# Gated mixing moved into the gather loop of a graph attention, on one core of a Trainium2 chip

## The chip, the cores and the metric

The kernel runs on one core of one Trainium2 chip. The core has five engines with queues of their own: TensorE (PE: matmuls; PEld is its weight load), VectorE (DVE), ScalarE (ACT), GpSimd (POOL) and SyncE (SP, which here only issues DMAs and passes signals). They meet at semaphores. The metric is the device time of one execution in microseconds; less is better.

## What is computed

Two layers over a graph of 6250 nodes and 206250 edges (sorted by destination), each: a graph operator plus a mixing operator, added to x, then a mixture of experts. The change is about the first layer's first half:

```
xn = layernorm(x)
x  = x + gnn(xn, edges) + mix(xn)

gnn:  h = xn @ W                       (8 heads of 32)
      e = leaky_relu(a1[src] + a2[dst])
      alpha = softmax of e over the edges of one destination
      out[dst] = sum over edges of h[src] * alpha   (+ bias)

mix:  context = softmax(K, over nodes)^T V          (one 32x32 block a head)
      out  = Q context
      gate = sigmoid(gelu(layernorm(xn) @ Wg1 + bg1) @ Wg2 + bg2)
      result = (out * gate) @ Wproj + bproj
```

Both are to within float32 accuracy; nothing of this differs between the two kernels.

## The kernel before

**Stages.** The program is a row of blocks, each ended by a barrier of all engines. `opening` reads x, writes the rows h (`h_dram`) and the turned, normalised x (`xt_dram`), and folds Q and the context into one matrix `wqc`. `mix_out` does the gated mixing alone. `attend` is the attention. Then come the experts, the relation rows, the relations' gather (`relations`, which like `attend` uses `report_groups` and `gather_groups`) and the last experts.

**`mix_out`** goes over the 49 blocks of 128 nodes in quads (four blocks, 512 columns), 13 of them. PE computes the hidden gate (`psG`), x times `wqc` (`psQ`) and the gate (`psV`); ACT does Gelu and Tanh; DVE multiplies (line 810); PE projects per block (line 753); DVE adds x and the bias (line 793) and SP stores to `x_dram`. x was read into `k.xb` by `opening`; POOL adds the biases to it and, once a block is done, sets its part of `k.xb` to zero (line 709, 49 memsets), because `attend` sums into `k.xb`.

**`attend`** first makes tables on DVE in a block of its own (lines 978 to 988), then the row of numbers `psN` on PE in another (`numbers`), and then runs the loop. Edges come in 202 groups of 1024 (8 tiles of 128). POOL gathers the rows h[src] of a group by 8 indirect DMAs (line 868) into a ring of 7 groups. A *step* handles a pair of a group and a block of destinations: 250 steps, T = 202 + 49 - 1. Four steps make a *turn* (U = 4).

In step t the engines work for several steps at once. DVE: waits `turned` (of PE's transposes); small operations on the maxima (1131 to 1164), ending in the exponents' arguments `arg`; with them `fade` (line 1108), which scales a block's sums by the correction of step t-1; then `hot` (1168, which destination each edge has, for step t+3), `scan` (1172), `add_up` (1113, adds the sums of step t-1 from `psS`), the edge types' part of the messages (1178), and the messages (1182). ACT: Exp of `arg` into the bank `psW` (1009), stages the next gathered rows (1015), and makes `hot_t` in two passes (1021, 1023). PE: first half of the sums of step t (1042), `spread_nodes` (915), the logits `psL` (1063, waits DVE's `shifts`), the maxima `psX` (1071, waits DVE's `marked`), two transposes (1076, 1080, which signal `turned`), and the second half of the sums.

**Written out or in a loop.** Each engine runs turns 1 to 61 as a hardware loop, `Fori(1, z.T // U)`. Steps -5 to 3 ahead of it and the last two steps, 248 and 249, are written out. In the loop, PE and DVE read the numbers of groups and blocks into registers once a turn (`Ahead`). Written-out steps read them with `one_of` wherever they are used. On PE that is inside the loop over j:

```
for j in range(G):
    pe.matmul(psL_v[:, j, :, :], hot_t[...],
              split[:, ds(block_no(2) * LW, LW)], ...)
```

so `block_no(2)` is read 8 times. `v.drain()` holds DVE's next instruction until all before it are done.

Of the kernel before, what the change touches and what calls it, by code (L numbers as in the profile page):

```python
# [5 lines left out]
P = 128  # L6
# [73 lines left out]
class Sizes:  # L80
# [4 lines left out]
    def __init__(self, n, e):  # L85
# [11 lines left out]
        self.NCH = -(-(self.T + 3 * U) // P)  # L97
        self.COLS = self.NGT * G
# [56 lines left out]
def opening(nc, z, S, k, mean, rstd, rstd2, ratio, wqc):  # L155
# [10 lines left out]
    with ExitStack() as c:  # L166
# [21 lines left out]
        blocks = sb("blocks", [P, nch * P], I32)  # L188
# [33 lines left out]
        with nc.Block() as block:  # L222
            @block.sync
            def _(sp):
# [11 lines left out]
                sp.dma_start(k.src_at[:], S["src"]).then_inc(of_late, 16)  # L236
# [7 lines left out]
                for b in range(NB):  # L244
# [10 lines left out]
                    if b == tables_at + 4:  # L255
                        sp.wait_ge(tab2, 16 * 2 * nch)
                        lines = k.table_dram.rearrange("q n o -> q (n o)")
                        sp.dma_start(k.last_pair[:], lines[0:1, :]).then_inc(tab3, 16)
                        sp.dma_start(k.pair_block[:], lines[1:2, :]).then_inc(tab3, 16)
                        sp.dma_start(blocks[:], lines[1, :].partition_broadcast(P)).then_inc(tab3, 16)  # L260
# [15 lines left out]
            def _(p):  # L276
# [12 lines left out]
                p.iota(k.pair_group[:], [[1, nch * P]], base=0, channel_multiplier=0)  # L289
# [300 lines left out]
        with nc.Block() as block:  # L590
            @block.vector
# [41 lines left out]
def mix_out(nc, z, k, S, wqc, ratio):  # L633

    NB = z.NB
    GH = S["L0_mix_Wg1"].shape[1]
    quads = [(lo, min(lo + 4, NB)) for lo in range(0, NB, 4)]
    NQ = len(quads)  # L640
    with ExitStack() as c:
        sem = c.enter_context(semaphores(nc, "mo_"))
        sb = lambda n, s, d=F32: c.enter_context(nc.sbuf_tensor("mo_" + n, s, d))
        xt = sb("xt", [P, NB, C])
        g1 = sb("g1", [P, KC, GH])
        g1s = sb("g1s", [P, KC, GH])
        g2 = sb("g2", [GH, C])
        wp = sb("wp", [P, KC, C])
        cols = sb("cols", [P, 3, KC])
        half = sb("half", [P, KC])  # L650
        bg1 = sb("bg1", [GH, 1])
        bg = sb("bg", [GH, 1])
        bias = sb("bias", [P, 2, C])
        hid = sb("hid", [GH, 2, 4 * P])
        gate = sb("gate", [P, KC, 4 * P])
        prod = sb("prod", [P, 2, KC, 4 * P])
        new = sb("new", [P, 4, C])
        psG = c.enter_context(nc.psum_tensor("mo_psG", [GH, 2, 512], F32))
        psQ = c.enter_context(nc.psum_tensor("mo_psQ", [P, KC, 512], F32))
# [2126 lines left out]
```

## Time and profile before

| what | us |
|---|---|
| median of 3 runs | 6431.17 (6430.95 to 6431.87) |
| the profiled execution, its own time | 6432.53 |
| its span in the profile | 6430.7 |
| granted TensorE clock, mean | 0.885 |
| opening | 0 to 249 |
| mixing alone (`mix_out`) | 249 to 409 |
| `attend`, tables and row of numbers | 410 to 419 |
| `attend`, first gather to last sum | 419.8 to 2509.0 |
| experts of the first layer | 2510 to 3070 |
| relation rows | 3070 to 3912 |
| relations and what is behind | 3912 to 6431 |

The stages' ends were read off the timeline of instructions; the profiled execution took 1.8 us more than its span, which lie around it. In the attention (420 to 2510) the engines' busy times are PE 1596.5, DVE 1823.0, ACT 697.3 and POOL 1532.4 us. A busy time there says little by itself: POOL is never idle for long, though it counts as busy 73% only, since 0.30 us stand between two of its gathers.

### The profile page before, as it was taken

Reading aid. Unit: us, or ns where it says so; the run is one execution under the profiler, and the core shown is the slowest. Engines: PE = TensorE matmul, PEld = TensorE weight load, DVE = VectorE, ACT = ScalarE, POOL = GpSimd, SP = SyncE. Lnnn points to the kernel's source line nnn. Section 1 sums busy time; section 2 is a strip of 40 time slices with the busy share of each in tenths; the row PEclk is TensorE's granted clock in tenths of the full one; section 3 lists DMA queues with packets and bytes.
Section 4 is the critical chain, followed back from the end, with each engine's and each line's share of the span. In section 5 each row is a group of like instructions: output and inputs, shape, how many; then the busy total and the mean of one; then the engine's idle time right before and its main releaser. Section 6 shows DMA issues by size and latency. Waiting matters only on the chain. (4 is left out here: it accounts for less than half of the span.)

```text
span 6430.7 us, 105194 instructions
## 1 busy us (share of the span) xinstructions
PE 4977.0 (77%) x26438; PEld 3591.3 (56%) x26691; DVE 4128.9 (64%) x9565; ACT 1548.3 (24%) x3076; POOL 3649.1 (57%) x3844
## 2 busy tenths in 40 slices
PE   5867777777777776799799997777777777766694
PEld 4535555555555555798544444655555555555583
DVE  5438999998989898435650003877777777666444
ACT  1213333333333333454433331000000000000341
POOL 3447777777777773603200004777777777776524
PEclk8978999989888887799999998888888888888597
DMA  4424444444444443423344443333333333333345
GB/s 144 125 72 109 113 113 113 113 113 113 113 113 113 113 112 117 143 77 103 106 149 169 174 171 126 109 109 109 109 109 109 109 109 109 106 105 96 131 147 151
DMA packets 367220, 762.40 MB, mean 119 GB/s; under 512 B 92003, under 2 KB 232321, under 8 KB 354241
## 3 DMA queue, kind: packets, MB, share of 16 engines
q0 software_dynamic: 175104, 491.59, 27.1%
q1 hardware_dynamic: 184912, 262.86, 12.1%
q10 hardware_dynamic: 7056, 6.43, 0.3%
q8 instruction: 39, 0.64, 0.0%
q14 instruction: 109, 0.89, 0.0%
HBM read 562.75 MB, written 199.66 MB: 119 GB/s over the span
## 5 line engine op out<-in xcount | busy, mean ns | idle before, releaser
L868 POOL DMA_INDIRECT rg_ring<-y_dram,src_at x1612 | 1528.3, 948 | 1265.2 <-POOLq L906 774.3
L868 POOL DMA_INDIRECT ga_ring<-h_dram,src_at x1612 | 1532.6, 951 | 507.9 <-issue 460.8
L1716 PE MATMUL rg_psS<-rg_ring,rg_hot_w 128*128 x4000 | 1148.1, 451 | 397.7 <-SPq L844 304.2
L1716 PEld LDWEIGHTS rg_psS<-rg_ring,rg_hot_w 128*128 128x128 f32 x4000 | 902.0, 230 | 640.2 <-issue 478.1
L1042 PE MATMUL ga_psS<-ga_msg,ga_hot 128*128 128x280 f32 x4000 | 1194.1, 455 | 46.1 <-DVE ga_msg L1182 38.1
L1042 PEld LDWEIGHTS ga_psS<-ga_msg,ga_hot 128*128 128x128 f32 x4000 | 850.0, 221 | 313.9 <-DVE ga_msg L1182 88.6
L1833 DVE TENSOR_SCALAR rg_hot_t<-rg_psB,pair_node,place 128x1024 bf16<-128x1024 f32 x253 | 338.4, 1338 | 586.0 <-PE rg_psB L915 586.0
L1521 PE MATMUL rr_psY<-rr_wr,rr_xt 128*128 128x512 f32 x1568 | 675.1, 593 | 4.6 <-DMA rr_xt<-x_dram 4.6
L1182 DVE SCALAR_TENSOR_TENSOR ga_msg<-ga_psW,ga_ring 128x2112 f32<-128x2112 f32 x251 | 587.3, 2340 | 0.0
L1521 PEld LDWEIGHTS rr_psY<-rr_wr,rr_xt 128*128 128x128 f32 x1568 | 298.4, 190 | 379.0 <-issue 373.9
L2261 PE MATMUL f_psH<-f_xt,f_now 128*128 128x128 f32 x2688 | 351.3, 281 | 48.9 <-DVE f_now L2554 37.9
L1800 DVE TENSOR_TENSOR rg_picked<-rg_psL,rg_rel 128x384 f32<-128x384 f32 x251 | 138.9, 553 | 359.5 <-PE rg_psL L1723 333.9
L2261 PEld LDWEIGHTS f_psH<-f_xt,f_now 128*128 128x128 f32 x2688 | 323.2, 194 | 66.2 <-DVE f_now L2554 43.6
L1506 ACT COPY rr_y<-rr_psY 128x512 f32<-128x512 f32 x392 | 229.7, 586 | 457.6 <-PE rr_psY L1521 457.6
L2100 POOL DMA_INDIRECT xg_dram<-f_row,f_pos x196 | 200.6, 1023 | 238.6 <-DVE f_pos L2426 180.1
L2271 PE MATMUL f_psO<-f_w,f_work 128*128 x1344 | 335.2, 386 | 0.6
L1168 DVE SCALAR_TENSOR_TENSOR ga_hot<-ga_psN,pair_node,dstf 128x1024 f32<-128x1024 f32 x253 | 323.7, 1279 | 8.6 <-issue 5.6
L1802 DVE SCALAR_TENSOR_TENSOR rg_hot<-rg_psN,pair_node,dstf 128x1024 f32<-128x1024 f32 x251 | 320.0, 1275 | 1.4 <-issue 1.4
L1009 ACT ACTIVATE ga_psW<-ga_arg 128x72 f32<-128x72 f32 x251 | 58.8, 234 | 1078.8 <-DVE ga_arg L1164 1078.8
L1829 DVE TENSOR_TENSOR rg_hot_w<-rg_hot,rg_psN 128x1024 f32<-128x1024 f32 x251 | 306.1, 1220 | 16.3 <-issue 0.4
L1023 ACT ACTIVATE ga_hot_t<-ga_apart,ones 128x1024 bf16<-128x1024 f32 x253 | 290.6, 1149 | 17.4
L1021 ACT ACTIVATE ga_apart<-ga_psB,ga_here 128x1024 f32<-128x1024 f32 x253 | 278.2, 1100 | 58.3 <-PE ga_psB L915 58.1
(403 smaller groups left out, 6694.3 us busy)
## 6 DMA issues: line engine op xcount, KB each, us to landing
y_dram<-rr_y SPq DMA_DIRECT2D x98, 1024.0 KB
f_x<-xg_dram SPq DMA_DIRECT2D x224, 128.0 KB
yg_dram<-f_work SPq DMA_DIRECT2D x224, 128.0 KB
ga_ring<-h_dram,src_at POOLq DMA_INDIRECT x1612
rg_ring<-y_dram,src_at POOLq DMA_INDIRECT x1612
rr_xt<-x_dram SPq DMA_DIRECT2D x98, 128.0 KB, 3.8
f_w<-L_ffn_W SPq DMA_DIRECT2D x16, 512.0 KB, 6.0
h_dram<-op_row SPq DMA_DIRECT2D x49, 136.0 KB, 1.8
```

What stands on the lines that cost most here:

```text
L868: p.indirect_dma_start(ring[:, (g % R) * G + j, :], None, table, bass.IndirectOffsetOnAxis(ap=rows[:, g * G + j:g * G + j + 1], axis=0)).t ...
L1023: act.activation(hot_t[:, (u + 3) % 2, :], apart[:], ACT.Relu, bias=k.ones[:, 0:1], scale=-1.0).then_inc(spent, 1)
L1042: o = pe.matmul(psS[:, u % 2, 0:MROW], hot[:, u, j, :], msg[:, u % 2, j, :], start=j == 0, stop=j == G - 1)
L1168: v.scalar_tensor_tensor(hot[:, (u + 3) % U, :, :], iota, k.pair_node[:, ds(t + 3, 1)], k.dstf[:, ds(group(3) * G, G)].unsqueeze(2).to_bro ...
L1182: v.scalar_tensor_tensor(msg[:, s1, :, 0:HC1].rearrange("p j (h w) -> p j h w", w=HW), w[:, s1, 0:G, :].unsqueeze(3).to_broadcast([P, G, H ...
L1521: t = pe.matmul(psY[:, q % 2, :], xt[:, u, kc * P:(kc + 1) * P], wr[:, kc, (part * YP + q) * 512:(part * YP + q + 1) * 512], start=kc == 0 ...
L1716: o = pe.matmul(psS[:, u % 2, 0:C], hot_w[:, u % 2, j, :], rows[:, j, :], start=j == 0, stop=j == G - 1)
L1802: v.scalar_tensor_tensor(hot[:, (u + 1) % 2, :, :], iota, k.pair_node[:, ds(t + 1, 1)], k.dstf[:, ds(group(1) * G, G)].unsqueeze(2).to_bro ...
L1829: v.tensor_tensor(hot_w[:, (u + 1) % 2, :, :], hot[:, (u + 1) % 2, :, :], w.unsqueeze(2).to_broadcast([P, G, P]), ALU.mult).then_inc(weigh ...
L1833: v.tensor_scalar(hot_t[:, (u + 3) % 2, :], psB[:], k.pair_node[:, ds(t + 3, 1)], k.place[:, 0:1], ALU.subtract, ALU.is_equal).then_inc(sp ...
L2261: t = pe.matmul(psH[:, u % 2, q * P:(q + 1) * P], now[:, u % 2, kc * HID + q * P:kc * HID + (q + 1) * P], xt[:, u % 2, kc * P:(kc + 1) * P ...
L2271: t = pe.matmul(psO[:, u % 2, 0:C], hidt[:, u % 2, q * P:(q + 1) * P], w2[:, ds((e * HC + q) * C, C)], start=q == 0, stop=q == HC - 1)
```

## The change

1. **`mix_out` is gone as a stage.** Its work is in `attend`'s loop, one block of 128 nodes to a turn, for turns 0 to 48. PE: `project` in the turn's first step, `ask` (6 matmuls) in the second, `weigh` (2) in the third, all between `psL` and `psX`. ACT: `keep` (scaled copy of the result and its store) and the load of the next turned block behind its own work in the first and second step, `curve` (Gelu) in the second, `squash` (two Tanh, and `lean`, a diagonal of 1/ratio) in the fourth, before its two passes, and the load of x's rows at the end. DVE: `multiply` at the end of the fourth step. The last sum, of x and bias, is two more matmuls with `lean` on PE and a scaled copy on ACT, no longer DVE's and POOL's.
2. **Banks.** The mixing needs a PSUM bank (`psM`). `psW` is given up: Exp writes its 72 numbers behind the 280 columns of sums, in the two banks `psS`. So ACT waits for the sums of step t-1 before Exp; and on DVE `fade` goes from the head of a step to behind `scan`, with a wait for `weights` ahead of it and a `v.drain()` between it and `add_up`.
3. **Loops.** Every engine's loop is cut in two. Turns 1 to 47 are a loop with the mixing, turns 48 and 49 (steps 192 to 199) are written out, turns 50 to 61 are a loop without it.
4. **Around it.** `k.xb` is zeroed by POOL in `opening`'s last block. `numbers` joins the tables' block, with the loads of the mixing's weights and some work on them. The index table `src_at` (812 KB) is read in `attend` by pieces of 8 groups into a ring of three, and whole only in the relation rows' stage. Some tables are shorter (262 numbers, not 384), `apart` is bf16.

```diff
-def mix_out(nc, z, k, S, wqc, ratio):
...
+            @block.gpsimd
+            def _(p):
+                for b in range(NB):
+                    p.memset(k.xb[:, b * XW:(b + 1) * XW], 0.0)
...
+        def w_of(u):
+            at = MROW + u // 2 % 2 * WW
+            return psS[:, u % 2, at:at + WW].rearrange("p (j h) -> p j h", j=G + 1)
...
                         act.wait_ge(args, now)
+                        act.wait_ge(summed, now)
                         act.nop()
-                        act.activation(w[:, (u + 1) % 2, :, :], arg[:, (u + 1) % 2, :, :], ACT.Exp).then_inc(weights, 1)
+                        act.activation(w_of(u + 1), arg[:, (u + 1) % 2, :, :], ACT.Exp).then_inc(weights, 1)
...
+                def ask(i):
+                    pe.wait_ge(xt_in, i * 16 + 16)
+                    if not isinstance(i, int) or i >= 1:
+                        pe.wait_ge(added, i)
+                    for kc in range(KC):
+                        pe.matmul(psG, g1[:, kc, :], xt[:, kc * P:(kc + 1) * P], start=kc == 0, stop=kc == KC - 1)
+                    for m in range(KC):
+                        for kc in range(KC):
+                            o = pe.matmul(psQ[:, m, :], wqc[:, kc, m * P:(m + 1) * P], xt[:, kc * P:(kc + 1) * P],
+                                          start=kc == 0, stop=kc == KC - 1)
+                    o.then_inc(asked, 1)
...
+                def project(i):
+                    pe.wait_ge(timed, i)
+                    for m in range(KC):
+                        pe.matmul(psO, prod[:, m, :], wp[:, m, :], start=m == 0, stop=False)
+                    pe.wait_ge(leaned, i)
+                    pe.wait_ge(rows_in, i * 16)
+                    pe.matmul(psO, lean[:], new[:], start=False, stop=False)
+                    pe.matmul(psO, lean[:], bias[:], start=False, stop=True).then_inc(projected, 1)
...
+                alone(-5, 0)
+                alone(0, U, 0)
+                with pe.Fori(1, NB - 1) as i, ExitStack() as held:
+                    turn(i, held, "m", i, i)
+                alone((NB - 1) * U, NB * U, NB - 1, NB - 1)
+                alone(NB * U, (NB + 1) * U, None, NB)
+                with pe.Fori(NB + 1, turns) as i, ExitStack() as held:
+                    turn(i, held, "")
...
-                    if before:
-                        fade(t - 1, u + 1, block_no(-1))
                     v.drain()
...
+                    if n1:
+                        v.wait_ge(weights, now)
                     if before:
-                        add_up(t - 1, u + 1, block_no(-1))
+                        fade(t - 1, u + 3, block_no(-1))
                     if n1:
                         g = group(1)
                         v.tensor_tensor(msg[:, s1, :, HC1:], psN[:, 0:REL].unsqueeze(1).to_broadcast([P, G, REL]),
                                         k.etf[:, ds(g * G, G)].unsqueeze(2).to_broadcast([P, G, REL]), ALU.is_equal)
-
-                        v.wait_ge(weights, now)
+                    if before:
+                        v.drain()
+                        add_up(t - 1, u + 3, block_no(-1))
+                    if n1:
...
+                    if u == 3 and make is not None:
+                        multiply(make)
```

How the instructions stand, DVE first, in the last step of a turn in the loop, from the arguments' end on. Before, where `psW` holds the exponentials and 1108 (`fade`) is higher up:

```order
L1149 TENSOR_TENSOR ga_both<-a 128x8
L1108 ISA
L1108 TENSOR_TENSOR xb<-xb,ga_psW 128x264
L1155 SCALAR_TENSOR_TENSOR ga_bent<-ga_both 128x144
...
L1172 SCALAR_TENSOR_TENSOR ga_scan<-ga_flags,ga_psI 64x128
L1113 TENSOR_TENSOR xb<-xb,ga_psS 128x280
L1178 REGISTER_ALU
L1178 TENSOR_TENSOR ga_msg<-ga_psN,etf 128x8x16
L1182 ISA
L1182 SCALAR_TENSOR_TENSOR ga_msg<-ga_psW,ga_ring 128x8x264
```

And the same place now:

```order
L1141 TENSOR_TENSOR ga_both<-a 128x8
L1145 SCALAR_TENSOR_TENSOR ga_bent<-ga_both 128x144
...
L1162 SCALAR_TENSOR_TENSOR ga_scan<-ga_flags,ga_psI 64x128
L1096 ISA
L1096 TENSOR_TENSOR xb<-xb,ga_psS 128x264
L1170 REGISTER_ALU
L1170 TENSOR_TENSOR ga_msg<-ga_psN,etf 128x8x16
L1101 TENSOR_TENSOR xb<-xb,ga_psS 128x280
L1176 ISA
L1176 SCALAR_TENSOR_TENSOR ga_msg<-ga_psS,ga_ring 128x8x264
L1104 REGISTER_ALU
L1105 SCALAR_TENSOR_TENSOR ga_prod<-ga_prod,ga_psM 128x256
```

`fade` (now 1096) stands behind `scan`, the types' part (1170) between it and `add_up` (1101), and `multiply` (1105) at the end.

ACT in the loop with the mixing, from the second step's passes to the third step's Exp:

```order
L948 ACTIVATE ga_hot_t<-ga_apart,ones 128x1024
L909 REGISTER_ALU
L911 ACT_TABLE_LOAD
L911 ACTIVATE ga_hid<-ga_psM,ga_bg 64x128
L914 ISA
L914 DMA ga_xt<-xt_dram 128x256
L722 ISA
L722 TENSOR_LOAD pair_group
L722 ISA x2
L929 REGISTER_ALU
L932 ACT_TABLE_LOAD
L932 ACTIVATE ga_psS<-ga_arg 128x72
```

Each turn with mixing has two loads of ACT's function table, one ahead of Gelu and one ahead of the next Exp; the kernel before has none in its loop.

PE in a step written out in the new turn 48 (step 192), where before the loop's one register served all eight matmuls:

```order
L722 TENSOR_LOAD pair_block
L722 ISA x2
L1035 ISA
L1035 MATMUL ga_psX<-ga_split,ga_hot_t 128x40
L1012 MATMUL ga_psM<-ga_wp,ga_prod 128x256 x2
L1015 MATMUL ga_psM<-ga_new,ga_lean 128x256
L1016 MATMUL ga_psM<-ga_bias,ga_lean 128x256
L1049 MATMUL ga_psX<-ga_peaks,ga_hot 128x8 x16
```

The first four rows are the last of eight such pieces, one for each matmul of `psL`; `project`'s four matmuls (1012 to 1016) stand behind them.

## Rows read from the trace of the kernel before

**Rows 1.** One line's instructions: the attention's gather on POOL (durations ns, starts us).

```profile
L868 POOL DMA_INDIRECT ga_ring<-h_dram,src_at x1612: 942/947/1186, 419.8 to 2448.0; - x180
```

**Rows 2.** Timeline, DVE: first operation of steps 4, 13, 85 and 248 (start, length, us).

```profile
526.89 0.23 DVE L1131 TENSOR_TENSOR ga_ends<-ga_psI,last 128x64 f32<-128x64 f32 x1 [2.12 <-PE ga_psI L1080]
...
598.38 0.20 DVE L1131 TENSOR_TENSOR ga_ends<-ga_psI,last 128x64 f32<-128x64 f32 x1
...
1165.83 0.21 DVE L1131 TENSOR_TENSOR ga_ends<-ga_psI,last 128x64 f32<-128x64 f32 x1
...
2479.41 0.21 DVE L1131 TENSOR_TENSOR ga_ends<-ga_psI,last 128x64 f32<-128x64 f32 x1
```

**Rows 3.** Timeline, the opening's last block, mixing's start, attention's start.

```profile
239.90 0.23 DVE L594 RECIPROCAL op_total<-op_psH 128x1 f32<-128x1 f32 x2 [3.35 <-PEq L492]
...
248.28 0.69 DVE L609 COPY wqc<-op_psT 128x512 f32<-128x512 f32 x1 [2.09 <-PE op_psT L628]
...
254.09 0.17 DVE L796 TENSOR_SCALAR mo_half<-mo_cols 128x2 f32<-128x2 f32 x1 [5.12 <-DMA mo_bg<-L_mix_bg]
...
260.29 0.43 DVE L803 TENSOR_SCALAR mo_wp<-mo_wp 128x512 f32<-128x512 f32 x1 [5.41 <-DMA mo_bias<-L_gnn_bias]
...
410.87 0.43 DVE L978 TENSOR_SCALAR a<-a,least 128x392 f32<-128x392 f32 x1 [2.79 <-PEq L50]
...
417.15 0.43 DVE L988 TENSOR_SCALAR ga_here<-pair_node,place 128x384 f32<-128x384 f32 x1
```

**Rows 4.** One line's instructions: the memsets of `k.xb` on POOL.

```profile
L709 POOL MEMSET xb<- x49: 328/332/345, 282.8 to 408.1; 128x280 f32 x49
```

**Rows 5.** Timeline, one ordinary step of the loop on DVE.

```profile
1010.11 0.16 DVE L1149 TENSOR_TENSOR ga_both<-a 128x8 f32 x1
1010.18 0.42 DVE L1108 TENSOR_TENSOR xb<-xb,ga_psW 128x264 f32 x1
1010.69 0.31 DVE L1155 SCALAR_TENSOR_TENSOR ga_bent<-ga_both 128x144 f32<-128x144 f32 x1
...
1012.68 0.40 DVE L1172 TENSOR_TENSOR_SCAN ga_scan<-ga_flags,ga_psI 64x128 f32<-64x128 f32 x1
...
1013.00 0.41 DVE L1113 TENSOR_TENSOR xb<-xb,ga_psS 128x280 f32 x1
...
1013.34 0.28 DVE L1178 TENSOR_TENSOR ga_msg<-ga_psN,etf 128x128 f32<-128x128 f32 x1
...
1013.54 2.34 DVE L1182 SCALAR_TENSOR_TENSOR ga_msg<-ga_psW,ga_ring 128x2112 f32<-128x2112 f32 x1
```

**Rows 6.** Timeline, DVE in step 0, which has no `fade`.

```profile
479.29 0.15 DVE L1149 TENSOR_TENSOR ga_both<-a 128x8 f32 x1
479.53 0.31 DVE L1155 SCALAR_TENSOR_TENSOR ga_bent<-ga_both 128x144 f32<-128x144 f32 x1
```

**Rows 7.** One line's instructions: the multiply of `mix_out` on DVE (durations ns).

```profile
L810 DVE SCALAR_TENSOR_TENSOR mo_prod<-mo_gate,mo_psQ x26: 286/687/689, 270.9 to 403.4; 128x512 f32<-128x512 f32 x24, 128x128 f32<-128x128 f32 x2
```

**Rows 8.** Timeline, ACT at the start of mixing: a load of its table, and Gelu.

```profile
259.98 1.28 ACT L715 ACT_TABLE_LOAD   x1 [22.98 <-PE mo_psG L743]
...
261.27 0.68 ACT L715 ACTIVATE mo_hid<-mo_psG,mo_bg 64x512 f32<-64x512 f32 x1
```

**Rows 9.** Timeline, ACT and PE in the step of rows 5.

```profile
1011.60 0.23 ACT L1009 ACTIVATE ga_psW<-ga_arg 128x72 f32<-128x72 f32 x1 [4.78 <-DVE ga_arg L1164]
...
1012.82 0.56 PE L1071 MATMUL ga_psX<-ga_peaks,ga_hot 128*128 128x8 bf16 x16 [0.88 <-DVE ga_hot L1168]
...
1013.51 0.30 PE L1080 MATMUL ga_psI<-ident,ga_sta 128*64 128x128 f32 x1
```

**Rows 10.** Timeline, PE at the end of mixing: 20 passes of 256 columns.

```profile
402.88 4.67 PE L753 MATMUL mo_psM<-mo_wp,mo_prod 128*128 128x256 f32 x20
```

**Rows 11.** Timeline, step 248, written out, on PE, and the start of step 249.

```profile
2489.40 0.21 PE L1063 MATMUL ga_psX<-ga_split,ga_hot_t 128*128 x1 [0.55 <-issue]
...
2492.21 0.23 DVE L1131 TENSOR_TENSOR ga_ends<-ga_psI,last 128x64 f32<-128x64 f32 x1 [2.33 <-PE ga_psI L1080]
```

More of the change, by code:

```diff
@@ L819, in report_groups @@
-def report_groups(nc, z, block, k, gathered, ready, room, freed, start, flags=None, flagged=None, late=None):
+def report_groups(nc, z, block, k, gathered, ready, room, freed, start, flags=None, flagged=None, late=None, src=None, indexed=None):
     @block.sync
@@ L852, in _, with gather_groups @@
                     flags_of(past // G + 2)
-def gather_groups(nc, z, block, k, table, rows, ring, gathered, room, go, halves=None):
+                if src is not None and past % G == G - 1 and past // G + 3 < batches:
+                    sources_of(past // G + 3)
+def gather_groups(nc, z, block, k, table, rows, ring, gathered, room, go, halves=None, indexed=None):
     @block.gpsimd
@@ new lines, in attend, with _ @@
+        weights_in = [(g2[:], S["L0_mix_Wg2"]), (wp[:], rows_of(S["L0_mix_Wproj"])),
+                      (bias[:], S["L0_mix_bproj"].partition_broadcast(P)),
+                      (new[:], S["L0_gnn_bias"].partition_broadcast(P))]
+        with nc.Block() as block:
+            @block.sync
+            def _(sp):
+                for dst, src in first:
+                    sp.dma_start(dst, src).then_inc(of_first, 16)
+                for dst, src in weights_in:
+                    sp.dma_start(dst, src).then_inc(of_weights, 16)
+                sp.dma_start(xt[:], k.xt_dram[0:P, :]).then_inc(xt_in, 16)
+                sp.wait_ge(of_sum, 1)
+                sp.dma_start(new[:], S["x"][0:P, :]).then_inc(rows_in, 16)
+            @block.tensor
+            def _(pe):
+                pe.wait_ge(of_first, 16 * len(first))
+                for kc in range(KC):
+                    t = pe.matmul(psM[0:MH, 0:2], g1[:, kc, :], cols[:, 1:3, kc], start=kc == 0, stop=kc == KC - 1)
+                t.then_inc(turned_bias, 1)
+                pe.matmul(psN[:, 0:P], k.ones[0:1, :], k.iota[0:1, :], start=True, stop=True)
@@ L1064, in step @@
                                       split[:, ds(block_no(2) * LW, LW)], start=True, stop=True)
+                    if u == 0 and close is not None:
+                        project(close)
+                    if u == 1 and make is not None:
+                        ask(make)
+                    if u == 2 and make is not None:
+                        weigh(make)
                     if n3:
```

375 lines of the change are left out of this document (158 added, 217 removed).

## The prediction, written before the changed kernel had run

> **What bounds the kernel now.** Only the stretch from the opening's end to the attention's last sum is touched. I read first the stages' ends on the timeline, then the gather's rows by line, then single steps of the attention on the timeline, DVE first and then who waits for it.
>
> Mixing is a stage of its own. DVE's last operation of the opening ends at 248.28 + 0.69 = 248.97, the attention's first begins at 410.87 [rows 3]: 161.9 us. That is what can be saved at most.
>
> In the attention two engines are near the edge, and the reader must see both. POOL issues 1612 gathers from 419.8 to 2448.0 [rows 1], 1.259 us apart, so 10.07 us a group; with 202 groups in 250 steps a turn of four steps can't take less than 10.07 x 202 / 250 x 4 = 32.5 us in the long run. DVE's own pace shows where the ring of gathered groups is full: from step 13 to step 85 the starts lie 1165.83 - 598.38 = 567.45 us apart [rows 2], 18 turns, so 31.53 us a turn. In it DVE does operation behind operation: the rows of one step [rows 5] have no idle time but that of the drains. Over the whole loop, from step 4 to step 248, it is 2479.41 - 526.89 = 1952.5 us for 61 turns [rows 2], 32.0 each: first DVE's pace, later the gather's. So what is put on DVE costs nothing up to some 0.5 us a turn late in the loop, and its full price above that.
>
> **The change, part by part.** The sum is made against the profiled execution, 6432.5 us.
>
> *Up to the first gather.* The opening's last block runs on DVE from 239.90 to 248.97 [rows 3]. POOL now sets k.xb to zero in it: 49 memsets of 0.33 us [rows 4]. Neighbouring short operations overlap by some 0.04 to 0.08 us (on DVE 0.40 us long, 0.32 to the next, rows 5), so 0.29 each, 14.2 us; POOL ends 5.1 us later than DVE did (between 4 and 7). Then the weights: the first five loads had landed at 254.09, the four more at 260.29 with half-megabyte loads of x ahead of them [rows 3]. The new stage has nine loads, the largest 256 KB, and only one block of x, behind them; so I take 256.5, nearer to the first, and 261.6 with the memsets. The new work on weights is some eight short operations, 1.5 us. The tables take 410.87 to 417.58, 6.7 us, as before, and from there to the first gather it was 2.2 us [rows 1, 3], of which I take 1.0 away for one block less (0 to 1.5). First gather: 261.6 + 1.5 + 6.7 + 1.2 = 271.0, against 419.8: **148.8 us saved** (145 to 152). POOL's additions of the bias and DVE's last sum go with it. The opening's index load is an eighth of its size; no row shows anything waiting for it, so 0.
>
> *A step on DVE.* At its head, `fade` stood between 1149 and 1155: 1010.11 to 1010.69, 0.58 us [rows 5]. Without it the same two are 479.29 to 479.53, 0.24 us apart [rows 6]. So -0.34. At its tail, from `scan` to the messages it was 12.68 to 13.54, 0.86. Now: 0.32 behind `scan`, `fade` 0.42 less the overlap of 0.07, the types' part in full, 0.28, since a drain follows, then a gap as behind `fade` now (10.60 to 10.69, 0.09), `add_up` to messages 0.34 as from 13.00 to 13.34: 1.38. So +0.52. Together **+0.18 us a step**, 0.72 a turn. The drain is the unknown: if the two cancel all but the drain it is 0.10, and a gap as large as an operation's latency makes it 0.40.
>
> *A turn with mixing on DVE.* `multiply` has 256 columns; 512 took 0.687 and 128 took 0.286 [rows 7], so 0.42, less the overlap 0.35. Its input comes from ACT's Tanh, early in the same step, 2 us or more before it: no wait.
>
> *ACT.* It waits 4.78 us for the arguments in an ordinary step [rows 9], so the extra 1 to 3 us a step are covered, but not what stands between the arguments and Exp. In the third step a table load stands there, since Gelu came before: 1.28 us [rows 8]. Arguments come 0.34 earlier than in rows 9, so Exp runs from 1011.26 + 1.28 + 0.03 = 1012.57 to 1012.80. DVE, its `scan` also 0.34 earlier, wants it at 1012.66: **0.2 us a turn** with the signal. Exp's other new wait, for the sums of step t-1, is one that DVE has today right behind the arguments, and the 31.53 us hold it.
>
> The row with its Gelu says that behind the load nothing more is paid, 259.98 + 1.28 to 261.27. The Trainium skill (ScalarE: Activation LUTs, What ACT_TABLE_LOAD costs) gives a switch about 1283 ns for the load and 1380 ns of drain beside it, 2.66 us together. Its load agrees with the row, the drain isn't seen there. By it a turn would cost 1.4 us more.
>
> So a turn with mixing takes 31.53 + 0.72 + 0.35 + 0.2 = **32.8 us** on DVE, above the gather's 32.5, and one without 32.25.
>
> *PE.* It waits 0.88 us for `hot` ahead of `psX`, and its last transpose ends at 1013.81 [rows 9], 2.0 us before the next step begins on DVE at 1015.8 (1013.54 + 2.34, rows 5, less the overlap). What is put between `psL` and `psX` has 2.9 us, 3.1 with DVE's longer step. Passes of 256 columns took 4.67 / 20 = 0.23 us [rows 10]; an f32 matmul is two. `project` is 8 such, 1.9 us; `ask` 12 of 128 columns, 2.8 at that price and less if the columns count; `weigh` 4, 0.9. Each fits, and the next step's wait of 0.88 us takes back what it inherits: 0 in the loop. x's rows for `project` are asked for at the end of the fourth step, more than 4 us ahead of their use: 0.
>
> *Written-out steps.* This is the dear part. Step 248 takes 2492.21 - 2479.41 = 12.8 us [rows 2, 11], and DVE waits 2.33 us for PE in it: each of the eight `psL` matmuls waits some 0.55 us for its issue, a read of the block's number. Eight more steps (192 to 199) are now written out: 8 x 12.8 = 102.4, where PE is the bound, so that mixing's matmuls count: two `project`, one `ask`, one `weigh`, 7.5 us. **109.9 us** for two turns. Steps 0 to 3 were written out before and get `ask` and `weigh`, 3.7 us. The ring can't help: there is nothing to catch up with later, as DVE stays the slower one.
>
> *The loop's sum.* 47 turns x 32.8 = 1541.6, plus 109.9, plus 12 x 32.25 = 387.0, is 2038.5 against 1952.5: +86.0. With 3.7 ahead and 0.5 for the last `fade`, which now waits for the sum: **+90.2 us**. The later stages: nothing; the index table is one of several loads that nobody waits for early.
>
> 6432.5 - 148.8 + 90.2 = 6373.9; the median was 1.4 below the profiled execution: **6372 us**, 0.9% faster. Of 149 us, 45 go to written-out steps, some 45 to `fade`'s place and the drain, a part of which the gather would have taken, and the rest to mixing on DVE.
>
> **The rivals.**
>
> *The drain costs more, 0.40 a step.* 236 loop steps x 0.22 = 52 us: 6424. For it: the new drain stands behind an operation that reads PSUM and ahead of another, which no row shows. Against: both drains that the rows show leave 0.09 us, behind `fade` and behind 1149 (479.44 to 479.53, rows 6). 0.15.
>
> *The gather stays the bound.* If the drain costs nothing, turns with mixing stop at 32.5: 6358. 0.08.
>
> *The table load costs its drain too.* 47 x 1.4 = 66 us: 6438. Against it is the row; for it that ACT had been idle there. The page named above is the source of that price. 0.05.
>
> *PE becomes the bound, and the kernel gets slower.* Place: `ask` in the second step, in the shadow of `project`'s delay from the first. It decides once what is put in passes 3.1 us with the lateness it inherits, about 1 us; at 2.8 us `ask` isn't far. Then DVE waits for `turned`: at 2 us a turn, 47 x 2 = 94, 6466. Against: a pass of 128 columns should take less than one of 256. 0.12.
>
> *The mixing isn't hidden, because it waits for its own loads.* If x's rows land 3 us after PE wants them: 141 us, 6513. 0.05.
>
> **How the numbers follow.** The forecast has 0.55 and its own range is 6345 to 6405. All but the last two and the table load end below 6431. A measurement can tell a change of about 0.2%, 12.9 us, from none. Faster by more: 0.55 + 0.08 + half of the 0.15 = 0.70; within: the other half and part of the table load, 0.12; slower: 0.18. The range goes from 6340 (the gather's bound with early weights) to 6445 (dear drain or table load), and leaves out the last two rivals.
>
> **What would show it.** First gather near 271. Starts of DVE's first operation: 32.8 us a turn up to step 191, then eight steps of 12.8 to 15, then 32.3. A gap of about 0.1 us ahead of `add_up`. Exp of the third step 1.3 us behind its arguments, and `fade` 0.2 us late there. POOL idle for room now and then. PE should not be what DVE waits for at a step's start, but in the written-out ones. Wrong it would be if that wait appears in the loop, or if written-out steps run at PE's loop speed.

## The result, and the profile of the changed kernel

Before: 6430.76 us (median of 19 runs, 6424.55 to 6433.76). After: 6418.24 us (19 runs, 6412.98 to 6421.01). The ratio is 0.9981, 95% interval 0.9974 to 0.9988: 12.5 us faster, where 59 were forecast. The time lies inside the range of 6340 to 6445, but most of the forecast gain is missing. The profiled execution of after has a span of 6416.2 us, 14.5 less than before; granted clock 0.892 against 0.885.

The head start is there. In the changed kernel 1123 is DVE's first operation of a step, 1096 `fade`, 1101 `add_up`, 1170 the types' part, 1176 the messages, 1105 `multiply`. Its gathers, one line's instructions (durations ns, starts us), which answer to [rows 1]:

```profile
L700 POOL DMA_INDIRECT ga_ring<-h_dram,src_ring x1612: 940/946/1172, 271.4 to 2414.6; - x180
```

Its memsets on POOL's timeline (start, length, us; before: [rows 4]):

```profile
240.22 13.45 POOL L595 MEMSET xb<- 128x280 f32 x49 [2.45 <-POOLq L493]
```

And DVE's timeline: the wait for the last weights, then the first operation of steps 4, 192, 200 and 248 (before: [rows 2, 3]):

```profile
262.28 0.43 DVE L858 TENSOR_TENSOR ga_bias<-ga_bias,ga_new 128x256 f32<-128x256 f32 x1 [12.95 <-DMA ga_new<-L_gnn_bias]
...
380.74 0.23 DVE L1123 TENSOR_TENSOR ga_ends<-ga_psI,last 128x64 f32<-128x64 f32 x1 [1.51 <-issue]
...
1958.97 0.23 DVE L1123 TENSOR_TENSOR ga_ends<-ga_psI,last 128x64 f32<-128x64 f32 x1 [0.63 <-issue]
...
2066.12 0.23 DVE L1123 TENSOR_TENSOR ga_ends<-ga_psI,last 128x64 f32<-128x64 f32 x1 [1.75 <-issue]
...
2467.42 0.22 DVE L1123 TENSOR_TENSOR ga_ends<-ga_psI,last 128x64 f32<-128x64 f32 x1 [0.84 <-issue]
```

The gather begins at 271.45 instead of 419.77, 148.3 us earlier. Then it is given back, almost all of it inside the loop. By these rows and those of before, in us:

| stretch | before | after | forecast of after |
|---|---|---|---|
| first gather to step 4 | 107.1 | 109.3 | 110.8 |
| 47 turns with mixing | | 1578.2 (33.58 each) | 1541.6 (32.8) |
| steps 192 to 199 | | 107.15 | 109.9 |
| 12 turns without mixing | | 401.3 (33.44 each) | 387.0 (32.25) |
| steps 4 to 248 together | 1952.5 | 2086.7 | 2038.5 |
| step 248 to the last sum's end | 29.54 | 29.55 | 30.0 |
| all behind it | | 2.5 less | the same |

148.3 - 2.2 - 134.2 + 2.5 is 14.4, the difference of the spans. The forecast's error is one row of this table: 134.2 instead of 86.0. And the 12 turns *without* mixing are as slow as those with it, so the mixing is not what costs.

Inside a turn, the last step is the odd one. The medians over the loop with mixing are 7.87, 7.84 and 7.84 us for the first three steps, against 7.71, 7.68 and 7.76 before in steps 4 to 87, where DVE sets the pace; the last one has 9.94, against 8.34. The end of a turn with mixing, on DVE's timeline:

```profile
1014.00 0.40 DVE L1162 TENSOR_TENSOR_SCAN ga_scan<-ga_flags,ga_psI 64x128 f32<-64x128 f32 x1
1014.33 0.40 DVE L1096 TENSOR_TENSOR xb<-xb,ga_psS 128x264 f32 x1
1014.65 0.28 DVE L1170 TENSOR_TENSOR ga_msg<-ga_psN,etf 128x128 f32<-128x128 f32 x1
1015.00 0.45 DVE L1101 TENSOR_TENSOR xb<-xb,ga_psS 128x280 f32 x1
1015.36 2.35 DVE L1176 SCALAR_TENSOR_TENSOR ga_msg<-ga_psS,ga_ring 128x2112 f32<-128x2112 f32 x1
1017.63 0.41 DVE L1105 SCALAR_TENSOR_TENSOR ga_prod<-ga_prod,ga_psM 128x256 f32<-128x256 f32 x1
1019.75 0.22 DVE L1123 TENSOR_TENSOR ga_ends<-ga_psI,last 128x64 f32<-128x64 f32 x1 [1.72 <-issue]
```

The end of one without mixing, in the same kernel:

```profile
2229.65 2.35 DVE L1176 SCALAR_TENSOR_TENSOR ga_msg<-ga_psS,ga_ring 128x2112 f32<-128x2112 f32 x1
2233.97 0.23 DVE L1123 TENSOR_TENSOR ga_ends<-ga_psI,last 128x64 f32<-128x64 f32 x1 [1.97 <-issue]
```

The end of a turn in the kernel before:

```profile
1028.94 2.34 DVE L1182 SCALAR_TENSOR_TENSOR ga_msg<-ga_psW,ga_ring 128x2112 f32<-128x2112 f32 x1
1031.90 0.22 DVE L1131 TENSOR_TENSOR ga_ends<-ga_psI,last 128x64 f32<-128x64 f32 x1 [0.62 <-issue]
```

Before, DVE is idle for 0.62 us between two turns; after, for 1.97, and `multiply` only fills a part of that: with it the idle time is 1.72. The releaser is "issue": by the profile DVE waits for no other engine. What its queue (DVEq) does in these places stands in the rows of the register loads (`Ahead`, 7 registers a load) and, in the changed kernel, of the new drain, durations in ns, start in us. Before:

```profile
L882 DVEq TENSOR_LOAD <-pair_group x1: 1637/1637/1637, 1027.9 to 1027.9; - x1
...
L882 DVEq TENSOR_LOAD <-pair_block x1: 1623/1623/1623, 1029.9 to 1029.9; - x1
```

After:

```profile
L1173 DVEq DRAIN  x1: 1512/1512/1512, 1013.4 to 1013.4; - x1
...
L714 DVEq TENSOR_LOAD <-pair_group x1: 1643/1643/1643, 1015.7 to 1015.7; - x1
...
L714 DVEq TENSOR_LOAD <-pair_block x1: 1623/1623/1623, 1017.7 to 1017.7; - x1
```

Before, the first load begins 1.0 us *ahead* of the messages' start (1027.9 and 1028.94), after 0.3 us *behind* it (1015.7 and 1015.36). In both the next turn's first operation begins 4.0 us behind the first load's start. In these rows the queue goes in order and ahead of the engine: it can reach the loads while DVE still works on what stands in front of them. The loads stand at the head of the next turn, so in the queue they come right behind the last step's messages (and `multiply`) and the loop's branch. The drain's row lasts 1.51 us in the queue, to 1014.9, which is when the types' part ends (1014.65 + 0.28), and the first load follows 0.8 us later. So the theory: **the new drain, between the types' part and `add_up`, holds the queue until that part is done, and with it everything queued behind, the next turn's register loads too.** What they then take beyond the messages' 2.3 us is idle time, once a turn.

Last, who is the bound now. POOL's waits for room in the ring (through SP's queue; us in total, times, longest), before:

```profile
POOL ga_ring L868 <- SPq L850: 47.1, 136, 6.0
```

After:

```profile
POOL ga_ring L700 <- SPq L675: 134.9, 52, 16.9
```

After, DVE is slower than the gather throughout: all turns of a kind are alike. Before it was so in the loop's first third only, where turns took 31.5 us, less than the gather's 32.5: there the loop used up what the gather had ahead. From step 88 on turns took 31.5 to 33.8.

### The profile page after: what moved, and what is told of

The parts are those of the page before. It is cut to its first block and busy times, and to the rows that moved or that the text cites. A ratio compares the mean times of both kernels' runs of the same rounds, so it can differ in the third digit from the quotient of the medians.

```text
span 6416.2 us, 108880 instructions
## 1 busy us (share of the span) xinstructions
PE 5023.4 (78%) x27462; PEld 3659.5 (57%) x27463; DVE 4131.4 (64%) x9540; ACT 1721.7 (27%) x3378; POOL 3608.7 (56%) x3795
## 5 line engine op out<-in xcount | busy, mean ns | idle before, releaser
L700 POOL DMA_INDIRECT ga_ring<-h_dram,src_ring x1612 | 1529.5, 949 | 632.4 <-issue 497.6
L987 PE MATMUL ga_psS<-ga_msg,ga_hot 128*128 128x280 f32 x4000 | 1123.3, 432 | 78.0 <-DVE ga_msg L1176 74.3
L987 PEld LDWEIGHTS ga_psS<-ga_msg,ga_hot 128*128 128x128 f32 x4000 | 796.6, 208 | 329.5 <-DVE ga_msg L1176 153.3
L1176 DVE SCALAR_TENSOR_TENSOR ga_msg<-ga_psS,ga_ring 128x2112 f32<-128x2112 f32 x251 | 590.0, 2351 | 0.0
L932 ACT ACTIVATE ga_psS<-ga_arg 128x72 f32<-128x72 f32 x251 | 58.8, 234 | 1166.4 <-DVE ga_arg L1154 1166.3
L1035 PE MATMUL ga_psX<-ga_split,ga_hot_t 128*128 x2016 | 111.0, 182 | 251.6 <-DVE ga_split L1152 188.0
L948 ACT ACTIVATE ga_hot_t<-ga_apart,ones 128x1024 bf16<-128x1024 bf16 x253 | 290.6, 1149 | 17.4
```

The lines of the kernel that those rows point to most:

```text
L700: p.indirect_dma_start(ring[:, (g % R) * G + j, :], None, table, bass.IndirectOffsetOnAxis(ap=at, axis=0)).then_inc((halves[j // HALF_G] i ...
L948: act.activation(hot_t[:, (u + 3) % 2, :], apart[:], ACT.Relu, bias=k.ones[:, 0:1], scale=-1.0).then_inc(spent, 1)
L987: o = pe.matmul(psS[:, u % 2, 0:MROW], hot[:, u, j, :], msg[:, u % 2, j, :], start=j == 0, stop=j == G - 1)
L1176: v.scalar_tensor_tensor(msg[:, s1, :, 0:HC1].rearrange("p j (h w) -> p j h w", w=HW), w_of(u + 1)[:, 0:G, :].unsqueeze(3).to_broadcast([P ...
```

## Experiments

**1 and 2. The same drain, in the kernel before, at two places.** Nothing of the change is in these two: no mixing, no cut loop, no shared bank. Edit (u == 3, the turn's last step, or u == 0, its first):

```diff
+                        if u == 3:
+                            v.drain()
                         v.wait_ge(weights, now)
                         v.scalar_tensor_tensor(
                             msg
```

> The kernel before with one v.drain() ahead of the messages in the last of a turn's four steps (u = 3), nothing else; the sum is not changed by it. Theory (the drain holds DVE's queue, and with it the register loads behind the last messages of a turn): the idle time ahead of the first DVE operation of a turn grows from 0.61 us to about 2.0, the two loads start about 0.3 us after the messages instead of 1.1 us before them, a turn takes 33.4 us instead of 32.0, and 61 turns cost 61 x 1.4 = 85 us: 6515 us (6500 to 6535). Rival (a drain costs only the operation's tail that it lays open, and the time of the changed kernel went elsewhere, into the cut loop or the PSUM banks now shared): 61 x 0.1 to 0.2 = 6 to 12 us, 6437 to 6443 us, with the idle time ahead of a turn unchanged.

> The kernel before with the same v.drain() in the first step of a turn (u = 0) instead of the last. Theory (it is what stands behind the drain in the queue that costs, the register loads): only the tail that the drain lays open, 0.1 to 0.2 us a turn, 6437 to 6443 us, idle time ahead of a turn still 0.6 us. Rival (a drain costs the same wherever it stands, because it empties the pipeline and the queue's lead is lost for good): the same price as in the last step, 6515 us if that one costs 1.4 us a turn.

Measured, against 6427.39 us for the kernel before in the same series: in the last step 6513.81 us, ratio 1.0132 (1.0115 to 1.0149), +86.4 us; in the first step 6431.21 us, ratio 1.0005 (0.9996 to 1.0015), +3.8 us, which can't be told from none. The same instruction costs 86 us at one place and next to nothing at the other. Where it stands last, DVE's timeline:

```profile
1024.44 0.28 DVE L1178 TENSOR_TENSOR ga_msg<-ga_psN,etf 128x128 f32<-128x128 f32 x1
1024.90 2.36 DVE L1184 SCALAR_TENSOR_TENSOR ga_msg<-ga_psW,ga_ring 128x2112 f32<-128x2112 f32 x1 [0.19 <-issue]
1029.42 0.23 DVE L1131 TENSOR_TENSOR ga_ends<-ga_psI,last 128x64 f32<-128x64 f32 x1 [2.17 <-issue]
```

And, in its queue, the drain and the first register load:

```profile
L1182 DVEq DRAIN  x1: 1819/1819/1819, 1022.9 to 1022.9; - x1
...
L882 DVEq TENSOR_LOAD <-pair_group x1: 1623/1623/1623, 1025.4 to 1025.4; - x1
```

The drain itself leaves 0.19 us ahead of the messages; the idle time ahead of the next turn is 2.17, near the changed kernel's 1.97, and the load begins 0.5 us behind the messages' start, 0.7 behind the drain's end. Where it stands first, that idle time is unchanged:

```profile
1032.67 2.34 DVE L1184 SCALAR_TENSOR_TENSOR ga_msg<-ga_psW,ga_ring 128x2112 f32<-128x2112 f32 x1
1035.64 0.23 DVE L1131 TENSOR_TENSOR ga_ends<-ga_psI,last 128x64 f32<-128x64 f32 x1 [0.63 <-issue]
```

Both rivals fall: the price needs neither the cut loop nor the shared banks, and a drain doesn't cost the same everywhere. The first place gave even less than the 6 to 12 us expected: its turns rose from 31.5 to 31.7 us where DVE is the bound, and behind step 88 the gather hid it. A turn takes 33.4 us with the last one, against the 31.5 of before's DVE-bound stretch. That is 1.9, where 1.4 was expected a turn over the whole loop's 32.0: some of before's loop is the gather's, and hid a part.

**3 and 4. A semaphore for the drain.** `faded` is raised by `fade`'s last instruction, and `add_up` waits for it:

```diff
-                                    ALU.mult)
+                                    ALU.mult).then_inc(faded, 1)
...
-                        v.drain()
+                        v.wait_ge(faded, now)
                         add_up(t - 1, u + 3, block_no(-1))
```

The first run has this alone; the second also has `fade` ahead of `scan`, so that `scan` and the types' part lie between the two.

> The changed kernel with the drain replaced by the semaphore alone (the fading multiply raises it, the last sum waits for it), the order of DVE's operations left as it is, with one operation (the types' part) between the two. Theory (what counts is how long the queue is held there, since the register loads of a turn stand behind it): the wait is over about as early as the drain's, only the tail of the types' part is no longer laid open, so most of the turn's price stays: 33.3 to 33.6 us a turn, 6400 to 6418 us. Rival (the drain instruction itself is dear, a semaphore in its place is not): as with the fading moved too, 32.5 us a turn, 6350 us.

> The changed kernel with the drain ahead of the last sum replaced by a semaphore which the fading multiply raises and the sum waits for, and the fading moved ahead of the scan, so that the scan and the other heads' work lie between the two. Theory (the drain holds the queue and its register loads): the idle time ahead of a turn falls from 1.72 to 1.97 us to about 0.6 to 0.9, a turn from 33.6 to about 32.4 us, 59 turns give back 59 x 1.1 to 1.2 = 65 to 70 us, and the time is 6350 us (6335 to 6375) unless PE or the gather becomes the bound earlier. Rival (the loop's longer turn comes from the cut loop or the shared banks, not from the drain): 6405 to 6418 us, with the idle time ahead of a turn still 1.7 us or more.

Measured: alone 6370.71 us, ratio to before 0.9914 (0.9897 to 0.9930); with `fade` moved 6350.32 us, 0.9878 (0.9861 to 0.9894). Against the changed kernel's 6418.24 that is -47.5 and -67.9. The kernel before had 6427.2 and 6427.4 in the series of these runs, where it had 6430.8 in the changed kernel's; with each taken against its own, it is -44.0 and -64.6.

The first is not what the theory gave: it expected 0 to 18 us. Each step got shorter, 7.68 us instead of 7.85, the last one by 0.22, and the turn is 32.9 instead of 33.6 (32.75 instead of 33.44 without mixing): 59 turns x 0.7 = 41 us. The rest isn't the edit's: the first gather began at 264.6 in this kernel, 6.9 us earlier than in the changed one, 272.2 in the second. (In the changed kernel and the five built on it, it lay between 264.6 and 272.2, so some us of any difference among them are the opening's.) So the drain has two prices: 0.16 us for what it lays open on the engine, in every step, and the held queue, once a turn. The expectation had seen only the second, and its rival, that the drain instruction is all of the price (6350 us), isn't met either.

The second met its 6350 us and its turn (32.5, with 32.4 expected), but in part by that same oversight. The idle time ahead of a turn was to fall to between 0.6 and 0.9 us; it fell from 1.72 to 1.34 only (from 1.97 to 1.68 without mixing). Of the 1.1 us that a turn gained, 0.65 are the drain's 0.16 in four steps, and some 0.4 are the queue's.

The end of a turn with the semaphore alone (1178 the messages, 1107 `multiply`):

```profile
1027.58 2.34 DVE L1178 SCALAR_TENSOR_TENSOR ga_msg<-ga_psS,ga_ring 128x2112 f32<-128x2112 f32 x1
1029.85 0.40 DVE L1107 SCALAR_TENSOR_TENSOR ga_prod<-ga_prod,ga_psM 128x256 f32<-128x256 f32 x1
1031.88 0.22 DVE L1125 TENSOR_TENSOR ga_ends<-ga_psI,last 128x64 f32<-128x64 f32 x1 [1.63 <-issue]
```

And with `fade` moved too:

```profile
1027.40 2.34 DVE L1178 SCALAR_TENSOR_TENSOR ga_msg<-ga_psS,ga_ring 128x2112 f32<-128x2112 f32 x1
1029.67 0.40 DVE L1107 SCALAR_TENSOR_TENSOR ga_prod<-ga_prod,ga_psM 128x256 f32<-128x256 f32 x1
1031.40 0.23 DVE L1125 TENSOR_TENSOR ga_ends<-ga_psI,last 128x64 f32<-128x64 f32 x1 [1.34 <-issue]
```

A semaphore's wait holds the queue too: the loads begin 0.3 us behind the messages' start with the semaphore alone, hardly sooner than with the drain, at the same time with `fade` moved, 1.0 ahead of it before. So it isn't the drain as such that holds the register loads but a wait this late in the turn for something just done, by either means; the semaphore in its place gives back 0.1 us of the loads' lead and the move of `fade` 0.3 more.

The Trainium skill (VectorE: DVE Perf Modes, The DRAIN you can't avoid) says that a semaphore between two operations of this engine costs nothing beside the pipeline's own flush, which happens anyway. The steps of 7.68 us, no more than the 7.68 to 7.76 of before, agree. These runs show beside it that an explicit drain costs 0.16 us more, and that either one holds what is queued behind it.

**5. The pieces' number read once.** In the changed kernel, on PE:

```diff
+                        pieces = split[:, ds(block_no(2) * LW, LW)]
                         for j in range(G):
                             pe.matmul(psL_v[:, j, :, :], hot_t[...],
-                                      split[:, ds(block_no(2) * LW, LW)], start=True, stop=True)
+                                      pieces, start=True, stop=True)
```

> The changed kernel with the block number that the pieces' matmuls of one step need read once, ahead of the eight matmuls, instead of once for each, in the eight steps that are written out (in the loops the numbers stand in registers anyway). Theory (the written-out steps take 13.4 us each against 8.4 in a turn because PE reads the number from memory eight times a step, some 0.77 us each, and DVE waits for it): 7 x 0.5 to 0.77 = 3.5 to 5 us less a step where nothing else holds it, 20 to 35 us in all, 6385 to 6398 us. Rival (DVE's own reads of numbers in these steps bound them): no more than 5 us, 6413 to 6418 us.

Measured: 6384.16 us, ratio to before 0.9931 (0.9915 to 0.9948), 34.1 us less than the changed kernel (30.7 with each against the before of its own series). PE in step 192 of the changed kernel, two of the eight matmuls, each behind its own read:

```profile
1964.16 0.19 PE L1035 MATMUL ga_psX<-ga_split,ga_hot_t 128*128 x1 [0.61 <-issue]
1964.93 0.19 PE L1035 MATMUL ga_psX<-ga_split,ga_hot_t 128*128 x1 [0.58 <-issue]
```

The same matmuls (in step 194) with the read hoisted, all eight in 0.37 us:

```profile
1971.11 0.37 PE L1036 MATMUL ga_psX<-ga_split,ga_hot_t 128*128 x8 [2.50 <-DVE ga_split L1153]
```

But steps 192 to 199 fell from 107.15 only to 91.9 us, 15.3 us; a further 8.0 came in steps 0 to 3, which are written out as well (52.4 to 44.5), 4.7 in a gather that began earlier, and the rest in the steps around. A step still takes 11.1 to 12.3 us. With PE out of the way, DVE's own reads are the bound, as its timeline shows in the idle time ahead of operations that use a number:

```profile
1968.82 0.23 DVE L1135 TENSOR_TENSOR ga_both<-ga_ring,ga_theirs 128x64 f32<-128x64 f32 x1 [0.89 <-issue]
...
1971.31 1.28 DVE L1159 SCALAR_TENSOR_TENSOR ga_hot<-ga_psN,pair_node,dstf 128x1024 f32<-128x1024 f32 x1 [0.87 <-issue]
```

So the total came within 1 us of the 6385 to 6398 expected, but by luck: the 20 to 35 us were to come from the eight steps, which gave 15.3, and the rest came from places that the expectation had not counted. The rival, that DVE's own reads bound these steps, was half right.

**6. All numbers of the written-out turns in two loads.** The semaphore and the moved `fade`, and for the turns 48 and 49 on PE and DVE the loop's way of reading:

```diff
                 def alone(lo, hi, make=None, close=None):
+                    if lo >= U:
+                        with ExitStack() as held:
+                            turn(lo // U, held, f"w{lo}", make, close)
+                        return
...
```

> The changed kernel with the semaphore and the fading ahead of the scan, and the two turns that are written out taking their numbers as a turn of the loop does, into registers with two loads a turn on PE and on DVE, instead of one read for each use. Theory (the written-out steps are dear only through single reads on PE and DVE): the 8 steps take about 65 to 68 us instead of 107, 6350 - 40 = 6310 us (6303 to 6320). Rival (what is written out is dear in itself, through the mixing's first and last parts or through code that is read for the first time): no better than with the pieces' read hoisted alone, 6350 - 34 + 15 = 6316 to 6335 us.

Measured: 6309.43 us, ratio 0.9818 (0.9802 to 0.9834), 40.9 us less than the run it is built on. The eight steps take 64.3 us (from 1906.41 to 1970.70), about two turns of the loop; in the run it is built on they took 107.1. Mixing's last parts and code that runs once cost nothing to speak of: all of the 43 us between the two were reads of single numbers.

**7. DVE's loads cut in two.** The same, and 5 + 5 registers at the head of the first and of the third step, in the loops and in the turns 48 and 49:

```diff
-                    groups = Ahead(v, held, "dve_g" + name, k.pair_group, 1, U + 3, z.NGT - 1)
-                    blocks = Ahead(v, held, "dve_b" + name, k.pair_block, -1, U + 3, z.NB - 1)
-                    groups.load(i * U)
-                    blocks.load(i * U)
+                    groups = Ahead(v, held, "dve_g" + name, k.pair_group, 1, 5, z.NGT - 1)
+                    blocks = Ahead(v, held, "dve_b" + name, k.pair_block, -1, 5, z.NB - 1)
                     for u in range(U):
+                        if u % 2 == 0:
+                            groups.load(i * U + u)
+                            blocks.load(i * U + u)
...
```

> The same with DVE's loads of a turn cut in two: 5 + 5 registers at the head of the first step and 5 + 5 at the head of the third, in the loops. Theory (the idle time ahead of a turn is the loads' end minus the messages' end, and what the loads take, 3.3 us for 7 + 7 registers, is too long for the messages' 2.3 us to cover): 10 registers take about 2.5 us, so 0.8 us less ahead of a turn, and 0 to 0.2 us more ahead of the third step; a turn falls from 32.5 to 31.7 to 31.9 us and 57 turns give 34 to 46 us beside the run without the cut: 6265 to 6276 us. Rival (the gather or PE becomes the bound first): no less than 10 us gained, with POOL no longer waiting for room in the ring or DVE waiting for the transposed scores; or none, if the idle time is the loop's own turn-around: 6308 us.

Measured: 6275.87 us, ratio to before 0.9766 (0.9749 to 0.9782), 33.6 us less than without the cut, just short of the 34 to 46 expected. The end of a turn on DVE (1182 the messages, 1111 `multiply`):

```profile
1010.91 2.34 DVE L1182 SCALAR_TENSOR_TENSOR ga_msg<-ga_psS,ga_ring 128x2112 f32<-128x2112 f32 x1
1013.18 0.40 DVE L1111 SCALAR_TENSOR_TENSOR ga_prod<-ga_prod,ga_psM 128x256 f32<-128x256 f32 x1
1013.94 0.23 DVE L1129 TENSOR_TENSOR ga_ends<-ga_psI,last 128x64 f32<-128x64 f32 x1 [0.35 <-issue]
```

Its first load, now of five registers:

```profile
L714 DVEq TENSOR_LOAD <-pair_group x1: 1203/1203/1203, 1010.9 to 1010.9; - x1
```

The idle time ahead of a turn is 0.35 us, less than the kernel before had. A turn takes 31.7 to 32.1 us up to step 144 (but for the first, 33.9); behind it turns of 32.5 to 34.4 appear, like those in the loop of before. There the gather is the bound again: ACT, which stages each gathered group, waits for SP's word that a group has landed (total, times, longest), behind 1497 us:

```profile
ACT ga_sta L939 <- SPq L669: 75.5, 33, 4.3
```

From 407 to 1497 us that wait is 2.2 us in all. Steps 4 to 248 take 1951.3 us, with the mixing in it, against 1952.5 before without.

Seven of the nine kernels side by side, from DVE's rows at one end of a turn (us; the first load's start relative to the messages' start, to a tenth as the rows have it):

| kernel | loads | messages | next turn | load ahead (-) or behind (+) messages | from load to next turn |
|---|---|---|---|---|---|
| before | 1027.9 | 1028.94 | 1031.90 | -1.0 | 4.0 |
| before, drain in first step | 1031.6 | 1032.67 | 1035.64 | -1.1 | 4.0 |
| before, drain in last step | 1025.4 | 1024.90 | 1029.42 | +0.5 | 4.0 |
| after | 1015.7 | 1015.36 | 1019.75 | +0.3 | 4.1 |
| semaphore | 1027.9 | 1027.58 | 1031.88 | +0.3 | 4.0 |
| semaphore, `fade` moved | 1027.4 | 1027.40 | 1031.40 | 0.0 | 4.0 |
| the same, loads cut in two | 1010.9 | 1010.91 | 1013.94 | 0.0 | 3.0 |

The last column is one number in six kernels and falls by 1.0 where the loads fall by 0.9 (from 1.65 + 1.62 to 1.20 + 1.18). Over all turns of the first loop the medians say the same. From the first load to the next turn it is 4.01 or 4.02 us in all eight kernels with 7 + 7 registers, the two left out of the table among them, and 3.04 with 5 + 5; from the second load's end to the turn's first operation it is 0.39 to 0.40 and 0.37. In these kernels a turn begins 4.0 us behind its first register load, whatever DVE has to do meanwhile, unless it waits longer for something else, as before does for the gather (up to 4.9). The idle time at a turn's end follows from it: in the changed kernel's turns without mixing 4.0 + 0.3 - 2.35 = 1.95 (1.97 in the rows), before 4.0 - 1.05 - 2.34 = 0.61 (0.62).

## Why the prediction was wrong, point by point

**The stage that is saved, right.** 148.8 forecast, 148.3 measured. That it agrees to 0.5 us is luck: the first gather lay anywhere between 264.6 and 272.2 in the six kernels with this opening. The terms inside it held less well: the memsets took 13.45 us instead of 14.2, the last weights landed at 262.28 instead of 261.6.

**Steps ahead of the loop, right in sign.** +3.7 forecast, +2.2 measured.

**A step on DVE, right.** +0.18 was forecast; measured is 7.85 against 7.68 to 7.76, +0.13 on average, with a gap of 0.07 us ahead of `add_up` in the rows above. Run 3 says that all of it, 0.16, is the drain: with the semaphore a step takes 7.68.

**The base of the turn: the step that failed.** "A turn with mixing takes 31.53 + 0.72 + 0.35 + 0.2" takes 31.53 us whole, with the 0.6 us of idle time at a turn's end in it, as though that were fixed. It isn't: it is the end of the register loads, which in before had a head start of 1.0 us. The drain was priced by what it opens on the engine, as rows 5 and 6 show for an older drain. What stands behind it in the queue was not listed. The older drains stand at the head of a step, with 4.6 us of work and more behind them in the step, so the queue has its lead again when it comes to the loads, and the rows could not show a loss. The missed term is +1.3 to 1.45 us in each of 59 turns: some 80 us. It belongs to the new order, a wait for `fade` or for the types' part this late in the turn, more than to the drain instruction: in run 4, with a semaphore and `fade` moved ahead, some 1.0 us of it is still there, and run 7 takes that away by shorter loads.

**Mixing on DVE and ACT, too dear.** `multiply` was to cost 0.35 a turn. It costs 0.1 (33.58 against 33.44), since it fills idle time ahead of the loads' end; had the loads not been late, it would have counted. The 0.2 for the table load ahead of Exp is 0. ACT's timeline in the second and third step of a turn:

```profile
998.85 1.15 ACT L948 ACTIVATE ga_hot_t<-ga_apart,ones 128x1024 bf16<-128x1024 bf16 x1
1000.01 1.28 ACT L911 ACT_TABLE_LOAD   x1
1001.31 0.36 ACT L911 ACTIVATE ga_hid<-ga_psM,ga_bg 64x128 f32<-64x128 f32 x1
1001.92 1.28 ACT L932 ACT_TABLE_LOAD   x1 [0.25 <-PE ga_psS L987]
...
1005.11 0.23 ACT L932 ACTIVATE ga_psS<-ga_arg 128x72 f32<-128x72 f32 x1 [1.90 <-DVE ga_arg L1154]
```

The load ahead of Exp runs as soon as the wait for the sums is over and doesn't wait for the arguments: it ends at 1003.20, 1.9 us before Exp has anything to do. The prediction had put it behind both. The same rows answer the rival with the load's own drain: Gelu's load begins 0.01 us behind the pass in front of it, and Gelu 0.02 us behind the load of 1.28, so this rival of 6438 us falls, as the row of before had said. The two errors, 47 x 0.45 = 21 us, hid a part of the missed term.

So of the 33.58 us, 31.5 are the old turn, 0.5 to 0.65 the drain and `fade`'s new place on the engine, 1.3 to 1.45 the late loads; `multiply` 0.1.

**What the gather hides: in the sum, but with too high a floor.** The 31.5 us hold only where the ring is full; before had 32.0 on average, so some 30 us of what DVE lost (59 x 0.5) had been waits for the gather. The forecast did take this in, as it summed whole turns against 1952.5. Its other figure was off: a floor of 32.5 us a turn by the gather. Run 7 has 1951.3 / 61 = 32.0 and the kernel before had 32.0 as well: the ring begins full, and the floor holds only from where that is used up. The rival of 6358 us ("the gather stays the bound") had its number from that floor. Run 4's turns of 32.5 us look like it but are DVE's own pace, with 1.3 to 1.7 us of idle time ahead of each; run 7's loop, at 31.98 us a turn with mixing, went below it.

**Written-out steps, right in size.** 109.9 forecast, 107.15 measured, by the mechanism named, the reads of one number. The prediction called it the dear part; it is the smaller one, since these eight steps took 65.35 us before: +41.8 of the 134.2. It took PE alone for the bound, and run 5 shows DVE's reads right behind.

**PE as the bound: no.** In the changed kernel's loop DVE never waits for the transposes. In one step with `project` its last transpose ended at 1027.54 and DVE began at 1027.68, and in about one turn in six the margin was below 0.2 us, so it was close (1.7 us was the usual); with shorter turns (run 6, 32.5 us) it still didn't decide.

**The loads of the mixing: no.** PE waits for no DMA in the loop.

**The drain's rival, 6424 us,** ended nearest to the result, with the wrong mechanism: a gap of 0.40 us in each step, where the gap is below 0.1 and the price comes once a turn.

## What to carry to other kernels

A wait or a drain costs twice: on the engine, the tail that it lays open, and in the queue, the lead of everything behind it. Before adding one, look what the queue still has to do before the engine's next work (register loads, a loop's turn-around, single reads), and whether the operation in front of it covers that without its head start. A long loop's idle time "issue" ahead of each turn is such a sum: it moves when a wait is put into its last step. A semaphore, raised early with other work between, gave back about half of what the change had cost a turn (33.6 to 32.5 us, with 31.5 before), and smaller loads most of the rest (31.8). And where code is taken out of a hardware loop, carry its way of reading numbers along: 8 steps cost 107 us with single reads and 64 with two loads a turn.

## What the runs showed of the hardware

- A load of registers took 1.00 us for 4 (on PE's queue), 1.19 to 1.20 for 5 and 1.62 to 1.65 for 7 (on DVE's): 0.21 us a register and about 0.15. The Trainium skill (Runtime: NRT & Kernel Launch, Instruction fetch mechanics) gives about 200 ns a register for the register loads of the launch; the kernel's own, in its loop, agree with 0.21.
- From the first of two such loads on DVE to the turn's first operation: 4.0 us with 7 + 7 registers, 3.0 with 5 + 5; so 0.6 to 0.75 us beside the loads themselves, 0.4 of it behind the second.
- A drain or a semaphore's wait holds the engine's queue: the drain's row lasts 1.51 us in the changed kernel and ends with the operation it waits for (both at 1014.9), and the register load follows 0.8 us later.
- The same `v.drain()` on DVE: +86 us in a turn's last step, +4 in its first, which can't be told from none.
- A load of ACT's table, right behind a pass of 1.15 us, cost its 1.28 us and nothing beside it: 0.01 us ahead of it and 0.02 to the next activation.
